# Group norm and output projection of a two-layer kernel put into one stage, written out, with six residual slots and three of normalised rows

## What is computed

```python
mean = y.mean(axis=(1, 3), keepdims=True)        # per sequence and head
var = y.var(axis=(1, 3), keepdims=True)
yn = (y - mean) / jnp.sqrt(var + EPS)
yn = yn.reshape(b, t, dm) * gn_weight + gn_bias
s = yn @ W_o.T
...
x = x + s * g            # g is already silu(feed-forward)
```

## Time and profile before

| | us |
|---|---|
| median of three runs | 1988.62 (1985.88 to 1989.11) |
| the profiled execution, device time | 1988.8 |
| span of its profile | 1987.0 |
| group norm, first to last VectorE instruction (lines 2247 to 2263) | 1893.5 to 1902.2 |
| output, first ScalarE instruction (line 2318) | 1903.25 |
| output, first and last multiplication by the gate (line 2304) | 1912.50 and 1980.45 |
| end of the last addition (line 2307) | 1982.93 |

### The profile page before, as it was taken

How to read it: one execution, slowest core, us unless ns; L and a number is a source line. 1 busy time by engine, 2 the same in 40 slices (tenths; PEclk the granted TensorE clock), 3 DMA queues, 4 the chain that set the end, 5 groups by cost and what they waited for, 6 DMA issues and landing times. The chain is left out here.

```text
span 1987.0 us, 64075 instructions
## 1 busy us (share of the span) xinstructions
PE 1414.6 (71%) x22151; PEld 978.0 (49%) x22152; DVE 1508.0 (76%) x3763; ACT 1192.5 (60%) x2964; POOL 1084.9 (55%) x1088
## 2 busy tenths in 40 slices
PE   3469999698896544555400079999997789999755
PEld 3435555465554433444300046666665456666544
DVE  7876777565664788778689879999996668888745
ACT  8647787556665466788656434444443567777643
POOL 6667777533333876678546612222222567777643
PEclk9999999899998677778655589999998999999878
DMA  8547666689994334334459833333332112222137
GB/s 253 180 130 182 186 193 177 171 186 203 216 219 135 109 116 145 115 117 140 126 140 196 161 71 66 65 63 61 65 65 51 46 44 53 53 53 53 44 108 231
DMA packets 453363, 247.78 MB, mean 125 GB/s; under 512 B 323517, under 2 KB 440832, under 8 KB 452736
## 3 DMA queue, kind: packets, MB, share of 16 engines
q1 hardware_dynamic: 440674, 210.71, 42.9%
q0 software_dynamic: 12576, 35.67, 5.9%
HBM read 79.52 MB, written 73.44 MB: 77 GB/s over the span
## 5 line engine op out<-in xcount | busy, mean ns | idle before, releaser
L197 PE MATMUL ps<-all_late,l_xq_T 128*128 128x352 f16 x1536 | 244.4, 317 | 173.3 <-DVEq L185 162.7
L197 PEld LDWEIGHTS ps<-all_late,l_xq_T 128*128 (+1 forms) x1536 | 147.9, 99 | 265.2 <-DVEq L185 163.1
L469 POOL TENSOR_TENSOR ffn_h<-ffn_fq_val,ffn_h 128x704 f16<-128x704 f32 x64 | 97.4, 1522 | 286.7 <-ACT ffn_h L464 286.7
L197 PE MATMUL ps<-l0moe_W,all_xT_all 128*128 128x16 f16 (+2 forms) x1152 | 190.3, 312 | 38.7 <-ACT all_xT_all L828 22.3
L647 ACT ACTIVATE ffn_th<-ps 128x352 f32<-128x352 f32 x128 | 59.3, 463 | 178.8 <-PE ps L197 178.8
L1362 POOL TENSOR_TENSOR all_late<-experts_se,all_mhalf 128x4 f32<-128x4 f32 (+1 forms) x77 | 76.3, 992 | 160.6 <-DVE experts_se L1471 148.7
L2211 POOL TENSOR_TENSOR all_late<-ret_pm,all_late 128x512 f16<-128x512 f32 x128 | 145.4, 1157 | 19.3 <-ACT all_late L2117 19.3
L197 PEld LDWEIGHTS ps<-l0moe_W,all_xT_all 128*128 (+1 forms) x1152 | 83.9, 100 | 120.6 <-ACT all_xT_all L828 26.0
L632 PE MATMUL ps<-all_late,ffn_hT 128*128 128x256 f16 x1088 | 131.7, 276 | 8.0 <-ACT l_xq_T L657 4.4
L1628 PE MATMUL ps<-all_ident,both_o 128*128 128x128 f16 x256 | 26.4, 265 | 148.5 <-ACT both_oT L1726 134.4
L197 PE MATMUL ps<-moe_E,experts_gT 128*128 x864 | 117.6, 276 | 16.5 <-DMA experts_gT<-slots_dram 12.0
(11 more groups left out here) (299 smaller groups left out, 4663.6 us busy)
## 6 DMA issues: line engine op xcount, KB each, us to landing
rows_dram<-all_late SPq DMA_DIRECT2D x72, 256.0 KB
ret_v<-ret_vpad SPq DMA_DIRECT2D x256, 64.0 KB
front_xin<-x SPq DMA_DIRECT2D x16, 512.0 KB, 4.4
x_dram<-front_x SPq DMA_DIRECT2D x16, 512.0 KB, 5.3
all_late<-x_dram SPq DMA_DIRECT2D x64, 128.0 KB
z_dram<-all_late SPq DMA_DIRECT2D x64, 128.0 KB
both_zin<-z_dram SPq DMA_DIRECT2D x16, 512.0 KB
both_xin<-x SPq DMA_DIRECT2D x16, 512.0 KB
```

Of the source, the lines that this page charges most:

```text
L197: mm = pe.matmul(out, lhs[a], rhs[b], start=first and n == 0, stop=last and n == 2, skip_group_check=True)
L469: eng.tensor_tensor(lo, self.shaped(t, hi), hi, ALU.subtract).then_inc(self.lo, 1)
```

## The change

Group norm and output become one phase, `phase_output`, and every engine's list in it is written out (`unrolled`).

- The barrier between the two phases and the priming of the semaphores are gone. ScalarE waits only for the semaphore `s_affine`; `affine` is a tile of this phase. The two small products of group norm write PSUM banks 6 and 7.
- The residual rows have six slots (`ROWS`). SyncE's list begins with loads; the store has skew 5. The addition writes its result over the residual rows, and the store reads them there. A load of group n from 6 on waits for the store of group n-6.
- The normalised rows, their high and low parts and the PSUM result have three slots (`TURNED`). The float32 normalised rows lie in `late`. `prod` keeps two slots, and only the addition reads it.
- The multiplication by the gate waits for the matmuls alone; the wait for the residual rows stands ahead of the addition; no instruction of VectorE waits for a store.
- In each step of SyncE's list the store comes ahead of the load.

The instructions that compute a group, their shapes and their number are the same. The core of the diff:

```diff
-def phase_output(nc, ps, yT_all, affine, w1, x1_dram, g1_all, out_dram):
+def phase_output(nc, ps, ystat, gn, blocks32, mhalf, yT_all, w1, x1_dram, g1_all, out_dram, late):
+    BC, ROWS, TURNED = BATCH * C, 6, 3
...
+        yn = late[:, 0:TURNED * C * G * P * 2].bitcast(F32).rearrange("p (u c k m) -> p u c k m", u=TURNED, c=C, k=G)
+        x1, prod = ph.sb("x1", [P, ROWS, G, D]), ph.sb("prod", [P, LAG, G, D])
...
         @block.sync
         def _(sp):
             def load(t):
-                sp.wait_ge(s_x, free(t))
-                sp.dma_start(x1[:, t.slot], token_groups(x1_dram)[t.n]).then_inc(s_in[t.slot], 16)
+                if t.n >= ROWS:
+                    sp.wait_ge(s_store[t.n % ROWS], 16 * (t.n // ROWS))
+                sp.dma_start(x1[:, t.n % ROWS], token_groups(x1_dram)[t.n]).then_inc(s_in[t.n % ROWS], 16)
             def store(t):
-                sp.wait_ge(s_x, done(t))
-                sp.dma_start(token_groups(out_dram)[t.n], prod[:, t.slot]).then_inc(s_store[t.slot], 16)
-            pipeline(sp, GROUPS, [(0, load), (2, store)])
+                sp.wait_ge(s_sum, t.n + 1)
+                sp.dma_start(token_groups(out_dram)[t.n], x1[:, t.n % ROWS]).then_inc(s_store[t.n % ROWS], 16)
+            unrolled(GROUPS, [(ROWS - 1, store), (0, load)])
...
             def add(t):
-                dve.wait_ge(s_o, done(t))
-                dve.wait_ge(s_in[t.slot], landed(t))
-                dve.wait_ge(s_store[t.slot], slot_free(t))
-                dve.scalar_tensor_tensor(prod[:, t.slot], ops[t.slot], 1 / WS, g1_all[:, bass.ds(t.n * G, G)], ALU.mult,
-                                         ALU.mult).then_inc(s_prod, 1)
-                dve.wait_ge(s_prod, done(t))
-                dve.tensor_tensor(prod[:, t.slot], prod[:, t.slot], x1[:, t.slot], ALU.add).then_inc(s_x, 1)
-            pipeline(dve, GROUPS, [(2, add)])
+                u = t.n % ROWS
+                dve.wait_ge(s_o, t.n + 1)
+                dve.scalar_tensor_tensor(prod[:, t.slot], ops[t.n % TURNED], 1 / WS, g1_all[:, t.n * G:(t.n + 1) * G], ALU.mult,
+                                         ALU.mult).then_inc(s_prod, 1)
+                dve.wait_ge(s_prod, t.n + 1)
+                dve.wait_ge(s_in[u], 16 * (t.n // ROWS) + 16)
+                dve.tensor_tensor(x1[:, u], prod[:, t.slot], x1[:, u], ALU.add).then_inc(s_sum, 1)
+            unrolled(GROUPS, [(0, add)])
...
         @block.scalar
+            act.wait_ge(s_affine, 1)
             def normalise(t):
+                u, b = t.n % TURNED, t.n // (TB // G)
+                if t.n >= TURNED:
+                    act.wait_ge(s_lo, t.n - TURNED + 1)
+                    act.wait_ge(s_o, t.n - TURNED + 1)
                 for c in range(C):
                     ...
                 ins.then_inc(s_yn, 1)
+                act.wait_ge(s_yn, t.n + 1)
+                act.activation(y16[:, u, 0], yn[:, u], ACT.Copy).then_inc(s_hi, 1)
+            unrolled(GROUPS, [(0, normalise)])
...
         @block.gpsimd
             def part_lo(t):
+                u = t.n % TURNED
+                pool.wait_ge(s_hi, t.n + 1)
+                if t.n >= TURNED:
+                    pool.wait_ge(s_o, t.n - TURNED + 1)
+                pool.tensor_tensor(y16[:, u, 1], yn[:, u], y16[:, u, 0], ALU.subtract).then_inc(s_lo, 1)
+            unrolled(GROUPS, [(0, part_lo)])
...
         @block.tensor
             def project(t):
+                u = t.n % TURNED
+                pe.wait_ge(s_lo, t.n + 1)
+                pe.wait_ge(s_hi, t.n + 1)
+                if t.n >= TURNED:
+                    pe.wait_ge(s_prod, t.n - TURNED + 1)
                 ...
+            unrolled(GROUPS, [(0, project)])
```

More of the change, by code:

```diff
@@ L2218, in _, with load, store @@
             pipeline(pool, TILES, [(4, states_lo), (2, keys_lo), (3, queries_lo), (4, scores_lo)], 3)
-def phase_group_norm(nc, ps, ystat, gn, blocks32, mhalf, affine):
-    BC = BATCH * C
-    with Phase(nc, "gn") as ph:
+def phase_output(nc, ps, ystat, gn, blocks32, mhalf, yT_all, w1, x1_dram, g1_all, out_dram, late):
+    BC, ROWS, TURNED = BATCH * C, 6, 3
+    with Phase(nc, "out") as ph:
         agg = ph.sb("agg", [P, BC, 2])
         m, d, e, ve, rstd = (ph.sb(n, [P, BC]) for n in "m d e ve rstd".split())
-        s_step, s_mean, s_e, s_var, s_ve, s_rstd, s_pass = ph.sems("step mean e var ve rstd pass")
-        block = ph.enter_context(nc.Block())
+        affine = ph.sb("affine", [P, 2, BC])
+        y16 = ph.sb("y16", [P, TURNED, 2, C, G, P], F16)
+        yn = late[:, 0:TURNED * C * G * P * 2].bitcast(F32).rearrange("p (u c k m) -> p u c k m", u=TURNED, c=C, k=G)
+        x1, prod = ph.sb("x1", [P, ROWS, G, D]), ph.sb("prod", [P, LAG, G, D])
+        s_step, s_mean, s_e, s_var, s_ve, s_rstd, s_affine = ph.sems("step mean e var ve rstd affine")
+        s_yn, s_hi, s_lo, s_o, s_prod, s_sum = ph.sems("yn hi lo o prod sum")
+        s_in, s_store = ([ph.sem(f"{n}{u}") for u in range(ROWS)] for n in ("in", "store"))
+        ops = [ps[:, 2 * u:2 * u + 2, :].rearrange("p b (k d) -> p (b k) d", d=D) for u in range(TURNED)]
+        block = ph.enter_context(nc.Block())
+        @block.sync
+        def _(sp):
+            def load(t):
+                if t.n >= ROWS:
+                    sp.wait_ge(s_store[t.n % ROWS], 16 * (t.n // ROWS))
+                sp.dma_start(x1[:, t.n % ROWS], token_groups(x1_dram)[t.n]).then_inc(s_in[t.n % ROWS], 16)
+            def store(t):
+                sp.wait_ge(s_sum, t.n + 1)
+                sp.dma_start(token_groups(out_dram)[t.n], x1[:, t.n % ROWS]).then_inc(s_store[t.n % ROWS], 16)
+            unrolled(GROUPS, [(ROWS - 1, store), (0, load)])
+            for u in range(ROWS):
+                sp.wait_ge(s_store[u], 16 * len(range(u, GROUPS, ROWS)))
         @block.tensor
@@ L2232, in _, with project @@
             pe.wait_ge(s_step, 2)
-            pe.matmul(ps[:, 0, 0:BC], blocks32[:], m[:], start=True, stop=True).then_inc(s_mean, 1)
+            pe.matmul(ps[:, 6, 0:BC], blocks32[:], m[:], start=True, stop=True).then_inc(s_mean, 1)
             pe.wait_ge(s_e, 1)
-            pe.matmul(ps[:, 1, 0:BC], blocks32[:], e[:], start=True, stop=True).then_inc(s_var, 1)
+            pe.matmul(ps[:, 7, 0:BC], blocks32[:], e[:], start=True, stop=True).then_inc(s_var, 1)
+            def project(t):
+                u = t.n % TURNED
[3 more added lines that the diff above has]
+                    pe.wait_ge(s_prod, t.n - TURNED + 1)
+                for k in range(G):
+                    for c in range(C):
+                        ins = split3(pe, ops[u][:, k], (y16[:, u, 0, c, k], y16[:, u, 1, c, k]),
+                                     (w1("out", c, 0), w1("out", c, 1)), c == 0, c == C - 1)
+                ins.then_inc(s_o, 1)
+            unrolled(GROUPS, [(0, project)])
         @block.vector
@@ L2250, in _ @@
             dve.wait_ge(s_mean, 1)
[L2251 removed]
+            step(dve.tensor_tensor(d[:], agg[:, :, 0], ps[:, 6, 0:BC], ALU.subtract))
             step(dve.tensor_tensor(e[:], d[:], d[:], ALU.mult))
@@ L2458, in layer1 @@
                                 ystat, yT_all, late)
-            phase_group_norm(nc, ps, ystat, gn, blocks2[:, 0:P], mhalf8, affine)
-            phase_output(nc, ps, yT_all, affine, w1, x1_dram, as_float32(xq_T), a["out"])
+            phase_output(nc, ps, ystat, gn, blocks2[:, 0:P], mhalf8, yT_all, w1, x1_dram, as_float32(xq_T), a["out"], late)
 def host_layout(i):
```

69 lines of the change are left out of this document (11 added, 58 removed).

## The result

The changed kernel took 1959.74 us in the median of four runs (1957.63 to 1962.12); before took 1987.25 (1981.94 to 1989.11) in the same set. The ratio is 0.9866 with a 95% interval of 0.985 to 0.9882. Two later sets with the same kernel gave 0.9857 (0.9842 to 0.9872) and 0.9876 (0.9859 to 0.9893). It was forecast faster, at 1967.7 us within 1963 to 1976.

A forecast was written before the change was run, and what follows sets the result against it. Bound: the latency of a store in a ring of two slots. First gate multiplication 1911.5 + 15 x 3.2 + 2.5 = 1962.0; with the tail 1966.1, with 1.8 outside the span 1967.9, from the median 1967.7 us; range 1963 to 1976.

The forecast's parts named there:

- The barrier: Between group norm and output: of 1.09 us before ScalarE starts, about 0.1 stays; gain 1.0 us.
- The first group: ScalarE's start to first gate multiplication: unchanged, up to 1.2 us later if TensorE's clock stays at the lower level.
- The period: Time per group in the output stage: 3.2 us in place of 4.53, with ends 2.9 and 3.7.
- The exclusion: Output stage: VectorE's addition and GpSimd's low part exclude each other; alternating takes 1.09 + 1.99 = 3.08 us a group.
- The tail: End of the last addition to end of the span: the same 4.07 us, up to 1.5 longer.
- The signs: What the profile after would show if right, such as a 3.1 to 3.3 us period and additions mostly over 2 us.
- The reference point: Ahead of the change: 20.9 us less than one profiled execution of 1988.8, or from the median, 1988.62, giving 1967.7.
- What bounds the kernel: Output stage before: VectorE waits for the store two groups back, landing in 5.79 us; period 4.53 us.
- DMA as the bound of the changed kernel: Rival, output stage: stores and loads get only 234 GB/s, 14.2 MB take 61 us, time 1979; chance 0.10.
- Code loading: Rival, written-out output stage: about three instruction-fetch gaps on TensorE cost 6.7 us, time 1974; chance 0.07.
- TensorE at the lower clock: Rival, output stage: at half clock a group takes up to 5.6 us, time 2005, slower than before; chance 0.03.
- Five loads and not six: SyncE's list: five loads precede the first store, since group 0's store comes before load 5; changes no number.

The follow-up runs named there:

- e1: The changed kernel with the gate product written back to PSUM and the addition reading it there; 1960.01 us, ratio 0.9846 to the kernel before.
- e7: The kernel before with each step's store ahead of its load in SyncE's list, nothing else; 1987.68 us, ratio 0.9987 to the kernel before.
- e3: The changed kernel with the result stored from the two slots of prod, VectorE waiting for stores again; 1967.84 us, ratio 0.989 to the kernel before.
- e2: The changed kernel with two slots of normalised rows, parts and PSUM results in place of three; 1977.04 us, ratio 0.9924 to the kernel before.
- e11: The changed kernel with three residual slots in place of six; 1969.88 us, ratio 0.9912 to the kernel before.
- e4: The kernel before with only the five lists of the output stage written out; 1988.72 us, ratio 0.9992 to the kernel before.
- e8: The changed kernel with the product in PSUM, eight residual slots and 46 matmuls with no reader before the first group; 1955.85 us, ratio 0.9824 to the kernel before.

## Why the prediction was right and wrong

**The barrier** (forecast 1.0 us): 1.07. Right.

**The first group** (kept at 9.25 us, with 1.2 us more for the range): 10.20. TensorE's clock stayed at 0.50 through the whole group, 5.34 us in place of 4.36. The range's term came true, almost in full (0.95 of 1.2; the range itself was widened by 1.0). The other profiles of the changed kernel had 9.07 to 10.20.

**The period** (forecast 3.2): this is the term of the sum that was mis-sized inside the stage. The exclusion's 3.08 us, worked out from two lengthened instructions, is what twelve of the fifteen intervals measured, to 0.01; with the first two (3.04 and 2.86) and the last (2.39, where GpSimd has nothing left to do), the mean is 3.01. I had added 0.1 for DMA "so near behind". DMA at a share of 87% was indeed near, and e1 shows that it binds at 2.63; at 3.08 no compute instruction of the output part waits for it. 15 x 0.19 are 2.8 us.

The whole-instruction lock of the Trainium skill (SBUF — State Buffer, "SBUF: two separate sides") would have given 3.35. The measured 3.08 decides for the rows. In them the addition ends 1.09 us after GpSimd's instruction and not 1.23, and GpSimd's ends 1.99 after the addition and not 2.12; that there is a lock, e1 bears out, where both instructions fell back to 1.23 and 2.14.

**The tail** (4.07 us behind the last addition): 1955.8 - 1951.85 = 3.95. Right.

**The signs.** No wait of the gate multiplication for DMA, ScalarE's early start and DMA busy in group norm came as named. Two did not: most additions were to take over 2 us, and they took 1.90 (the period came out at 3.08 all the same); and the granted clock was 0.87 while the second group ran and 1.00 only from the third on.

**The stage in sum**: 72.6 forecast, 70.47 measured, which was within the range's bounds for it (2.9 to 3.7 a period).

**The reference point** is the step that failed: it is what put the result outside the range. The sum stood on one profile, in which group norm began at 1893.5, and on a median of three runs. I took both as fixed, and the range held nothing for the phases ahead. The sixteen profiles, with nothing changed ahead of group norm but 64 bytes of placement in some, put that start between 1885.0 and 1898.2. The profile after began at 1885.3, which alone is 8.2 us; with the start forecast its time would have been 1965.8, inside the range. For the median of 1959.74 the same can be estimated: if 1.8 us outside the span and a stage of 70.0 to 70.5 are taken off, group norm began at 1887.4 to 1887.9, where the forecast, 1967.7, had 1893.3. So 5.4 to 5.9 of its 8.0 us of error lie ahead of the change and 2.1 to 2.6 in the stage. Why the phases ahead took less, chance or placement, stays open.

The stage before, which I took as 93.5, took 94.9 to 95.7 in the three later profiles of it. Of this 0.3 to 0.7 us lie in the first group, the rest in the period (4.58 to 4.65). The cause is not shown: TensorE's matmuls took less time in these profiles (296 to 297 ns in the mean) than in the first (301).

**What bounds the kernel** ("the latency of a store held in a ring of two slots"): half right. The profile named the store, and the wait was there. But the sentence on the loads, "that gives nothing by itself, since no wait of VectorE was for a load", was wrong: e7 took the load out of the store's way, and the wait went to the load at the same period. e3 shows that with deep rings elsewhere the store's two slots cost only 0.36 us a period; e2 that two slots of the other ring cost 0.95, e11 that three residual slots cost 0.49. In the kernel before two transfers hung on one addition, and the stage was bound by the landing of the second, whichever it was; the ring of normalised rows stood close behind, at 3.96. Putting back any one of the three (the residual slots only to three) brought a part of the loss back, and only the kernels with all of them deepened had 3.01. The sum came out because the change did deepen all. No run has two residual slots with the other rings deep, so what these alone cost is not shown.

**The rivals.** DMA as the bound of the changed kernel: no, 286 GB/s were moved, not 234. Code loading: no, e4 and the profile after have no matmul with an "issue" wait in the stage. Here the Trainium skill's "mostly hidden" (Runtime: NRT & Kernel Launch, "Instruction fetch mechanics") agrees with the trace, at 3.08 us for 24 matmuls and 24 weight loads. TensorE at the lower clock: no, 0.99 from 1904 us to the end of the additions. Five loads and not six: so it was, at no cost.

## What to carry to other kernels

When a wait is named as the bound, work out the round of every ring beside it (a ring is a buffer's slots in rotation, a round the time from one use of a slot to the next). If two have nearly the same length, the profile shows only the one that comes last, and shortening that one can move the wait to the other without moving the time, as in e7. The pace after such a change could here be worked out from a pair of instructions that lengthened each other in the trace before. For a time in absolute numbers, take the spread of the untouched phases from more than one profile before giving a range.

## What the hardware showed that I had not expected

- A VectorE instruction with one operand in PSUM and one in SBUF wasn't held up by GpSimd: the addition took 1225 ns for 128x1024 float32 in e1 beside GpSimd's running low part, against 1763 in the mean with both operands in SBUF. Writing the product in place to PSUM cost little: 1232 ns for the gate multiplication against 1213.
- 24 matmuls of 128x256 back to back take 2.62 us at full clock, against 2.79 for a group with a pause ahead of it (e1 and the changed kernel).
- A shift of all tiles by 64 bytes a partition changed the busy share of the DMA engines between 1400 and 1450 us from between 0.32 and 0.34 to between 0.26 and 0.29 at nearly the same bytes, in all sixteen profiles, while TensorE's busy time in the same 50 us stayed at 49.2 to 49.3.
- 46 matmuls without a reader, 7.8 us in time that TensorE stood idle anyway, brought its granted clock to 1.00 by the first group (e8). The first gate multiplication came 7.75 us after ScalarE's start, 1.3 to 2.5 us sooner than in the five profiles of the changed kernel (9.07 to 10.20).
